# Expert tiles of 128 rows: when TensorE's sequencer computes the register addresses of the expert weights

## The reference, cut to what matters

```python
shared = jnp.maximum(normed @ sw1 + sb1, 0.0) @ sw2 + sb2
probs = jax.nn.sigmoid(flat @ router_w.T)
scores, idx = jax.lax.top_k(probs, TOPK)          # 2 of 8 experts for each token
h = jnp.maximum(jnp.einsum('td,edh->teh', flat, ew1) + eb1[None, :, :], 0.0)
eo = jnp.einsum('teh,eho->teo', h, ew2) + eb2[None, :, :]
routed = jnp.einsum('teo,te->to', eo, comb)       # comb is 0 where an expert was not chosen
```

## Time and profile before

| | |
|---|---|
| median of 3 runs | 979.03 us (979.03 to 979.5) |
| span of the profiled execution, first to last instruction | 975.2 us |
| PE busy | 906.3 us, 93% of the span |
| PEld busy | 695.5 us, 71% |
| ACT busy | 626.9 us, 64% |
| DVE busy | 601.4 us, 62% |
| POOL busy | 466.4 us, 48% |
| mean granted TensorE clock | 0.981 of full speed |

### The profile page before, as it was taken

How to read it: one execution, slowest core, us unless ns; L and a number is a source line. 1 busy time by engine, 2 the same in 40 slices (tenths; PEclk the granted TensorE clock), 3 DMA queues, 4 the chain that set the end, 5 groups by cost and what they waited for, 6 DMA issues and landing times.

```text
span 975.2 us, 26284 instructions
## 1 busy us (share of the span) xinstructions
PE 906.3 (93%) x9049; PEld 695.5 (71%) x9050; DVE 601.4 (62%) x1199; ACT 626.9 (64%) x1029; POOL 466.4 (48%) x660
## 2 busy tenths in 40 slices
PE   3789899998999889999999999999999999999995
PEld 1444555555455546878998989989899987788885
DVE  8766799889898755865435444444443332327975
ACT  4778898888888776542655665556545544456753
POOL 5454566877768655474134444353434434311311
PEclk9789999999999899999999999999999999999998
DMA  5112223433323245587772112121212111139651
GB/s 171 66 66 93 93 100 103 141 121 138 115 83 121 99 169 200 192 292 265 265 248 65 55 65 68 52 71 49 77 44 71 52 60 61 51 100 290 221 162 44
DMA packets 69811, 116.98 MB, mean 120 GB/s; under 512 B 7808, under 2 KB 46080, under 8 KB 69600
## 3 DMA queue, kind: packets, MB, share of 16 engines
q1 hardware_dynamic: 52352, 81.51, 25.1%
q10 hardware_dynamic: 10896, 16.40, 5.7%
q0 software_dynamic: 6480, 17.97, 5.1%
HBM read 68.67 MB, written 47.18 MB: 119 GB/s over the span
## 4 chain that ended last, share of the span: by engine, by line
PE 66%; POOL 10%; DVE 9%; ACT 7%; issue 6%; DMA 0%; ACTq 0%; POOLq 0%; DVEq 0%; SPq 0%
PE hb L1815 25%; PE yb L1831 24%; PE pv_bank L1603 4%; PE yb L1706 3%; ACT prob L862 2%; PE hb L1669 2%; POOL xg_rows L731 2%; PE slot L1581 2%; PE tr L1689 2%; PE ma L1616 1%; PE slot L1590 1%; POOL nat L693 1%; POOL rsum L682 1%; POOL y L759 1%; POOL vv L710 1%
## 5 line engine op out<-in xcount | busy, mean ns | idle before, releaser
L1035 ACT ACTIVATE hf<-hb,b 128x256 f32<-128x256 f32 (+1 forms) x392 | 155.3, 453 | 210.9 <-PE hb L1815 205.2
L1815 PE MATMUL hb<-xgT,wts 128*128 128x256 f16 (+1 forms) x1872 | 219.1, 263 | 2.7 <-ACT hf L1035 2.7
L1831 PE MATMUL yb<-wts,hh 128*128 x1704 | 215.3, 273 | 0.0
L1458 DVE TENSOR_TENSOR hh<-hf,hh 128x1024 f16<-128x1024 f32 (+1 forms) x98 | 118.5, 1213 | 151.2 <-ACT hh L1040 119.7
L1815 PEld LDWEIGHTS hb<-xgT,wts 128*128 x1872 | 177.8, 98 | 25.4 <-issue 4.3
L797 POOL DMA_INDIRECT y_tok<-yb,dest x71 | 77.1, 1085 | 235.4 <-DVE yb L1470 225.2
L1831 PEld LDWEIGHTS yb<-wts,hh 128*128 128x128 f16 x1704 | 166.5, 98 | 21.1
L862 ACT ACTIVATE prob<-slot 128x1024 f32<-128x1024 f32 x160 | 162.3, 1043 | 24.1 <-PE slot L1590 23.1
L1040 ACT ACTIVATE hh<-hf 128x1024 f16<-128x1024 f32 (+1 forms) x98 | 97.6, 996 | 3.1
L731 POOL DMA_INDIRECT xg_rows<-xnh,sl_i x64 | 76.1, 1189 | 16.2 <-issue 13.9
L1581 PE MATMUL slot<-stk 64*128 64x128 f16 (+3 forms) x512 | 63.5, 306 | 16.2 <-ACT prob L862 10.4
(11 more groups left out here) (238 smaller groups left out, 1499.3 us busy)
## 6 DMA issues: line engine op xcount, KB each, us to landing
wts<-in_w_all SPq DMA_DIRECT2D x19, 512.0 KB
stage<-in_w_all SPq DMA_DIRECT2D x16, 512.0 KB
w_split<-chunk_hl SPq DMA_DIRECT2D x16, 512.0 KB
wts<-y_tok SPq DMA_DIRECT2D x32, 256.0 KB, 4.7
xg<-xg_rows ACTq DMA_DIRECT2D x30, 264.0 KB
wts<-w_split SPq DMA_DIRECT2D x3, 2048.0 KB
xTf<-in_xT SPq DMA_DIRECT2D x8, 512.0 KB, 4.1
xin<-in_x SPq DMA_DIRECT2D x8, 512.0 KB, 4.4
```

The costliest lines, as they stand in the source:

```text
L1035: act.activation(hf[:, c, 0:size], hb[c // 2][:, (c % 2) * TT:(c % 2) * TT + size], ACT.Relu, bias=bias, scale=1.0 / WS).then_inc(S("relu_ ...
L1458: dve.tensor_tensor(hh[:, par, 1, cs, 0:size], hf[:, cs, 0:size], hh[:, par, 0, cs, 0:size], ALU.subtract).then_inc(S("h_lo"), 1)
L1815: ins = pe.matmul(hb[hc // 2][:, (hc % 2) * TT:(hc % 2) * TT + size], weights(e, c, w, hc * P, P), xgT[:, par, x * DC + c, 0:size], start= ...
L1831: ins = pe.matmul(ybank[par][:, j * D:(j + 1) * D], hh[:, par, x, hc, P * j:P * j + P], weights(e, DC + hc * D // CH, w, hc * D % CH, D), ...
```

## The change

`both` gets a call ahead of each group of six hidden products (one `hc`). The call uses no address in a product: it only makes the builder compute the addresses at that point, four of the hidden weights and two of the output weights of block `hc`. The products then find them computed. Nothing else is changed; the order of the products, the waits that are asked for and the data are the same. Steps below 31 and from 38 on are not touched.

```diff
+                def addresses(e_in, e_out, hc, n_out):
+
+                    for c in range(DC):
+                        for w in range(2):
+                            pe.lower_ap(weights(e_in, c, w, hc * P, P), for_matmul_weights=True)
+                    for w in range(2):
+                        pe.lower_ap(weights(e_out, DC + hc * D // CH, w, hc * D % CH, D))
+
                 def both(i, e_in, e_out):
 ...
                     for k in range(N_IN):
+                        if k % (DC * len(PIECES)) == 0:
+                            addresses(e_in, e_out, k // (DC * len(PIECES)), n_out)
                         hidden_product((i + 1) // 2, (i + 1) % 2, e_in, k)
                         for m in range(k * n_out // N_IN, (k + 1) * n_out // N_IN):
                             output_product(i // 2, i % 2, e_out, m)
```

## The result

| | before | after |
|---|---|---|
| median | 979.26 us (979.03 to 979.73, 4 runs) | 972.84 us (970.73 to 974.33, 4 runs) |
| profiled execution | span 975.2 us | 974.11 us, span 972.4 us |
| seven steps of `both`, from the first transpose of step 31 | 52.02 us | 44.23 us |
| from the first product of step 38 to the end | 117.64 us | 117.63 us |

The change makes the kernel faster. The recorded ratio of after to before is 0.9928, interval 0.9909 to 0.9947. The forecast was 969.9 us; the measured time lies 2.9 us above it and inside the range of 967.6 to 975.6 us. The forecast gain was 9.1 us. Where the change acts the trace shows 7.8 us. The medians lie 6.4 us apart and the two profiled spans 2.8 us. What is missing in the spans arises ahead of the routed part, in this one execution; for the medians that is likely and not shown.

A forecast was written before the change was run, and what follows sets the result against it. PE's sequencer was taken to bound steps 31 to 37: 40.4 streaming + 1.0 starts + 1.3 wait = 42.7 us instead of 51.79 us. The 9.1 us gain from 979.03 us gives 969.9 us, range 967.6 to 975.6 us.

The forecast's parts named there:

- The floor: Steps 31 to 37: array streaming of products and transposes alone needs 40.4 us of the 51.79 us.
- The group: Nine products in `both`: sequencer needs 3 x 0.11 + 9 x 0.018 = 0.49 us, below the array's 0.655 us.
- Rival A: Steps 32 to 37: a product costs the sequencer 0.053 us, no lead builds up; 6.2 us a step, 972.7 us; 16%.
- rival B: Address instructions in `both`: one with six operations costs 0.2 us, group stays 0.76 us; gain 2.8 us, 976.2 us; 10%.
- The lead: Inside a step: the sequencer gets 19 products ahead of the array, 1.4 us of cover for the next start.
- the count with 38 entries: PE's queue: 19 products, each with a weight load; with 38 the forecast sum stays as it is.
- The starts: Starts of steps 31 to 37: nearly hidden, 0.15 us a step left, 1.0 us for seven.
- its 0.45 us of rest: Step 31: time that is no streaming, 8.53 us against 8.08 us.
- The one wait: First output product of step 34: waits once for DVE's half, behind POOL and ACT's load; 1.3 us, between 0 and 2.
- the wait in front of the L1831 product: Step 33 to 34: the expected sign of the single 1.3 us wait, with DVE's `hh` as its releaser.
- Behind step 37: Late stretch after the changed steps: everything as it was, some 9 us earlier, so the gain reaches the end.
- Rivals C and D: C: stalls before groups in `both`, +4.6 us, 983.6 us, 7%. D: ACT or late DVE cancels gain, 978 to 979 us, 6%.

The follow-up runs named there:

- pairs: Changed kernel with each two-address instruction just ahead of the first product that uses it, not in front of the group: 967.66 us against 974.69 us before.
- ahead: Kernel before with its single-address instructions kept, each computed one product earlier than its use: 975.26 us against 974.69 us before.
- incs: Changed kernel with four semaphore increments behind each group's addresses, three of them instructions of their own: 983.67 us against 974.69 us before.
- adds_early: Changed kernel with POOL's additions to `rs` in every third step instead of every fourth: 967.46 us against 976.36 us before.
- again: The changed kernel timed once more, unchanged: 967.13 us against 974.69 us before.

## Why the prediction was right, and where it was off

**What bounds these steps** was right: the sequencer, by its number of instructions. pairs, ahead and incs agree on it, each from another side. ACT, named by the profile, was not the cause.

**The floor** of 40.4 us was a little low. From the starts in the trace a product takes 0.110 and 0.055 us, a pair in step 31 0.165 us. That is 7.92 us for step 31, five steps of 5.50 and one of 5.28 us, with step 31's own transposes 0.22: 40.9 us, where the forecast counted so has 40.6 us.

**The group** was forecast at 0.49 us, and takes 0.44 us. Its two terms were both wrong and cancel: the six-operation instruction is 74 ns long and 0.132 us apart, not 58 ns and 0.11 us, and a product costs at most 5 ns, not 18. It fits that in the kernel before the next three-operation instruction starts 0.124 us later whether one product or two stand between. Rival A needed 53 ns a product, rival B 0.2 us an instruction; neither holds. Rival A's 972.7 us are next to the measured median, and still its mechanism is wrong: it asked for steps of 6.2 us, and steps 32, 35 and 36 take 5.6 to 5.7 us. A time alone would have confirmed the wrong cause.

**The lead** was forecast from the 19 products of the earlier trace rows. In the kernel after, counted in the trace whenever the sequencer begins the addresses of a group, the products not yet started grow by about 3 a group and stop at 17, in all steps but step 33, which has the wait in its middle. So some 17 products are the most that it gets ahead here, about 1.2 us of streaming: the count with 38 entries was the right one to keep, and the 2.3 us of cover with 64 were not to be had.

**The starts** were forecast at 0.15 us a step. From transposes to first product, less the 0.22 us of the transposes, the trace after has 0.05, 0.04, 0.17 and 0.10 us in steps 32, 33, 35 and 36, 0.09 us on average. Step 31 has 0.37 us. This is the step of the sum that failed there: I took its 0.45 us of rest for pace, of which 0.3 us would go. They do go, and the dearer front of the first group, behind two experts' numbers instead of one, takes them back.

**The one wait** came in step 34, from the chain of POOL and ACT that was named, at 1.26 us against 1.3 us, and its end is the forecast one: DVE's `hh` ends at 832.06 us. What the prediction did not see is the second way of the same chain, through the row load and the transposes. It lays the start open for 1.12 of the 1.26 us and takes the place of the wait in front of the L1831 product. Had the load come in time, the output product would by these times have waited for `hh` as forecast. That the size fits is luck in part. On the clock of before (5.00 us less) `hh` ends at 827.06 us and not at 826.65 us, and PE would have wanted it at about 825.8 us and not at 825.3 us; both are late, as step 31 gained nothing, and the errors cancel.

**What was missing**: DVE's `hh` stretched by POOL's addition, 0.73 us on PE in step 37, which adds_early shows by taking it away, and 0.2 us of a wait for `hh` in the middle of step 33. I had asked whether DVE has enough time, by its usual duration, and not who would now run beside it. In the kernel before that addition ran from 847.45 us and met the `hh` of 848.58 us for its last 0.15 us only; 1.3 us of shift of the one engine against the other made the meeting full.

Against the forecast of 42.7 us, with step 31's transposes 42.9, the sum is: step 31 +0.35, step 33 +0.25, step 34 -0.12, step 35 +0.10, steps 36 and 37 +0.71, step 32 -0.02. Together +1.3 us: 44.2 us.

**Behind step 37** all moved rigidly, 117.64 and 117.63 us. Rivals C and D are refuted: no gap stands in front of the groups, and what was won reaches the end.

**Around the span** I counted 3.8 us, by taking the median for the time of the profiled execution. It is 1.7 us: 974.11 - 972.4. The error drops out of the forecast, which is 979.03 less the gain.

## What to carry to other kernels

Before asking how long an engine's instructions take, count what its sequencer must issue for each group of work, at the distance from start to start; where that is above the streaming time, halve the number of instructions and do not merely move them. Then keep the first product of each stage free of preparation, since the lead won inside a stage pays for only one start of it. When one engine gets faster, go through the pairs of engines whose instructions will now run at the same time, and not only through the buffers.

## What the runs showed of the hardware

- Distances on TensorE's sequencer from start to start: a FUSED_REGOPS with three operations 0.124 us or more (46 ns long), one with six 0.132 us (74 ns), a semaphore increment 0.151 us (51 ns, in incs); a product without an address at most 5 ns. The same six-operation instruction between products, in pairs, stands 0.152 us from the next.
- A transpose or product with an unmet wait holds the sequencer: TENSOR_LOAD starts at 830.53 us with the transposes that waited, and the L1859 behind the product that waited until 849.53 us starts at 849.54 us.
- The sequencer got at most 17 products ahead of the array in the kernel after, each with its weight load.
- A DVE instruction with two inputs in SBUF gets longer beside a POOL addition, by nearly the time that both run. With all of the 1.28 us inside, it is 1.27 us; in again the `hh` at 817.61 us overlaps an addition for 0.36 us and takes 0.92 instead of 0.69 us. In the 256-row tiles it is 0.95 us for an overlap of 1.08 us. Here is DVE there in the kernel after, one `hh` with the addition beside it and one without:

```profile
521.02 2.17 DVE L1458 TENSOR_TENSOR hh<-hf,hh 128x1024 f16<-128x1024 f32 x1 [1.00 <-issue]
523.64 1.22 DVE L1458 TENSOR_TENSOR hh<-hf,hh 128x1024 f16<-128x1024 f32 x1 [0.45 <-ACT hh L1040]
```

And POOL at that time:

```profile
520.83 1.27 POOL L803 TENSOR_TENSOR rs<-rs,b2s 128x512 f32<-128x512 f32 x1
```

The Trainium skill (GPSIMD Engine Reference, section Specifications) says that GpSimd shares its SBUF interfaces with VectorE and contends with instructions that have two SBUF inputs. The trace agrees, with 1.96 against 0.69 us beside an addition of 1.28 us. By that rule a wait like that of step 37 could have been looked for, had the steps after the change been laid over POOL's; its price stands in the trace, in the 256-row tiles of the kernel before too.
